# Which engine makes four 128x512 sums of the hidden blocks in 13 of 48 units of a two-layer network on one core

## Chip, cores and metric

The kernel runs on one core of one Trainium2 chip. The metric is the device time of one execution in microseconds, lower is better. Three runs of the kernel before took 1935.4, 1935.69 and 1937.14 us (median 1935.69).

## Reference, cut to what matters

```python
x = x + L0(x, itok_B_0_2, wi, wo, swi, swo, g1, g2)    # x: (2, 2048, 512) float32
x = x + (einsum('bsd,bdh->bsh', x, W[cat]) + b[cat])   # one 512x512 matrix for each batch entry

def L0(x, label, wi, wo, swi, swo, g1, g2):            # D = 512, F = 2048
    s0 = relu(x @ swi[0]) @ swo[0]                     # shared network 0
    s1 = relu(x @ swi[1]) @ swo[1]                     # shared network 1
    eo = relu(x @ wi[label]) @ wo[label]               # chosen by a label for each batch entry
    w = softmax(relu(concat(eo[:, 0], s0[:, 0], s1[:, 0]) @ g1) @ g2)
    return eo * w[0] + s0 * w[1] + s1 * w[2]
```

## The kernel before

**Work.** The 4096 tokens are cut into four blocks ("supers") of 1024, the hidden width of each of the three networks into four slices of 512. One super, network and slice make a unit N; there are 4 x 12 = 48. The two products of a unit (up into the hidden layer, down out of it) are done by a seven-product scheme for 2x2 blocks: instead of eight block products, seven products of sums of blocks. The up product is done in two halves, n = 2N and 2N+1, of seven products each; the down product has seven for both halves together. Each operand is split into a high part (rounded, made by ScalarE, "ACT") and a low part (the remainder, made by VectorE, "DVE"), and TensorE ("PE") runs three matmuls for each tile pair: high by high, high by low, low by high.

**Hidden blocks.** Of each half, ACT and DVE bring four hidden blocks out of PSUM: `relu_11`, `relu_12`, `block_22` with `relu_22`, `block_21` with `relu_21`. DVE's `block_22` adds a copy `w` to a bank and writes `hid` (line 1332); `block_21` adds a copy `u` and writes `HT` (line 1341). The down products need four sums of these blocks, made by `hidden_sum` (line 772, its instruction in line 790): sum 0 = h22 - h12, sum 1 = sum 0 + h11, sum 2 = h12 - h11, sum 3 = h21 - sum 1. Each is 128x512 for one half. In every unit but unit 0, GpSimd ("POOL") makes the four sums of half 0 and DVE those of half 1. `sums_made` (line 766) names the semaphore and the count that tell of a sum; ACT's `hidden_high` and DVE's `hidden_low` (HH and HL, both halves in one 128x1024 instruction) wait for both halves.

**Weight blocks.** The first time a weight set is used, the kernel makes its sums and its high and low parts on the chip and stores them; later units load them. These are the prepared units: 0 to 11 and 32 to 35. There DVE also makes the sums of the up blocks (`up_sums`, 128x256) and all low parts (`up_low` into WU, `down_low` into WD), ACT all high parts, and GpSimd the four sums of the down blocks (`down_sums`, lines 792 to 807, 128x512, into PDS).

**Order.** There is no planner: each engine has its order written out. A pass m of the loops runs the up products of unit m+1 and the down products of unit m. The prediction calls it step m. In it a = 2(m+1) and b = a + 1 are the two up halves. PE's order is two up products, one down product, and so on seven times. On DVE a step begins with an addition of a down product into ACC (line 1310), then sums 0, 1 and 3 of unit m's half 1, `up_low` of a (late part), `up_sums`, low parts, an addition, sum 2, low parts, `up_low` of b (early part), `block_22(a)`, low parts, an addition, `block_21(a)`. The second half of the step has the same two blocks of b. ACT goes on from `block_21` with `relu_21` (line 952), `relu_12` (line 959) and `first_product` (line 924, a copy of one bank over another, for which a product of PE waits). `up` makes product 1 of a half wait for `block_21` of the half before, product 2 for `first_product`, product 6 for `block_22`.

GpSimd's loop (line 848) in pass m: sum 3 of unit m's half 0; sums 0 and 1 of unit m+1's half 0; two sums of down blocks if unit m+1 is prepared; sum 2; the other two sums of down blocks. So its first sums run in the second half of the step before. A sum may only be written when the down product of the unit before that used its place has been made.

Of the kernel before, what the change touches and what calls it, by code (L numbers as in the profile page):

```python
# [23 lines left out]
STEPS = SUPERS * STEPS_SUPER  # L24
# [37 lines left out]
LO_ORDER_END = [0, 1, 6, 2, 3, 4, 5]  # L62


T_COUNT = [(1, 2, 3, 4), (1, 2, 4, 3)]


def super_of(N):
    return N // STEPS_SUPER


def net_of(N):
    return N % STEPS_SUPER // STEPS_NET
# [6 lines left out]
def prepared(N):  # L80

    return 0 <= N < STEPS and (super_of(N) == 0 or (super_of(N) == 2 and net_of(N) == 2))
# [30 lines left out]
def ends_super(N):  # L113

    return N == 0 or N < STEPS - 1 and N % STEPS_SUPER == STEPS_SUPER - 1


def high_index(N, i):
# [28 lines left out]
def begins(N):  # L147

    return slice_of(N) == 0 and (super_of(N) % 2 == 0 or net_of(N) == 0)
# [11 lines left out]
def add_count(N, i):  # L161

    before = ADDS * (N - BEGUN[N]) + 2 * BEGUN[N]
    return before + ({4: 1, 5: 2}[i] if begins(N) else i)


def begin_count(N, i):
    return SUMS * BEGUN[N] + BEGINS[i]
# [44 lines left out]
def build(nc, xT, expert_id, category_id, wi, wo, swi, swo, g1, g2, W, bias, out):  # L213
# [13 lines left out]
    with ctx:  # L227
        def sem(name):
            return ctx.enter_context(nc.semaphore(name))
# [124 lines left out]
        s_T = [sem("hidden_sums_0"), sem("hidden_sums_1")]  # L354
# [393 lines left out]
        def ahead_sum(eng, s, q):  # L748

            done = 4 * (s - 1)  # L750
            if q == 0:
                eng.wait_ge(s_al, 48 * s)
                dst, x, y, op = XS[:, 2, :], XS[:, 2, :], XS[:, 1, :], ALU.subtract
            elif q == 1:
                eng.wait_ge(s_aT, done + 1)
                dst, x, y, op = XS[:, 1, :], XS[:, 1, :], XS[:, 0, :], ALU.subtract
            elif q == 2:
                eng.wait_ge(s_aT, done + 2)
                dst, x, y, op = XS[:, 0, :], XS[:, 2, :], XS[:, 0, :], ALU.add
            else:  # L760
                eng.wait_ge(s_al21, 16 * s)
                eng.wait_ge(s_aT, done + 3)
                dst, x, y, op = XS[:, 1, :], XS[:, 1, :], XS[:, 0, :], ALU.subtract
            eng.tensor_tensor(dst, x, y, op).then_inc(s_aT, 1)

        def sums_made(N, half, which):

            if half == 0 and N > 0:
                return s_T[0], 4 * (N - 1) + T_COUNT[0][which]
            return s_T[1], 4 * N + T_COUNT[1][which]  # L770

        def hidden_sum(eng, N, half, which):

            before = PRODUCTS * (N - 1)
            part = half if N > 0 else slice(0, 2)
            h11, h12, h22 = (hid[:, q, part, :] for q in range(3))
            if N > 0:
                eng.wait_ge(s_dn, before + (3, 2, 4, 5)[which] + 1)
            if which == 0:
                eng.wait_ge(s_relu, 4 * (2 * N + half) + 4)  # L780
                dst, p, q, op = HT[:, 3, part, :], h22, h12, ALU.subtract
            elif which == 1:
                eng.wait_ge(*sums_made(N, half, 0))
                dst, p, q, op = HT[:, 2, part, :], HT[:, 3, part, :], h11, ALU.add
            elif which == 2:
                dst, p, q, op = HT[:, 4, part, :], h12, h11, ALU.subtract
            else:
                eng.wait_ge(*sums_made(N, half, 1))
                dst, p, q, op = HT[:, 5, part, :], HT[:, 1, part, :], HT[:, 2, part, :], ALU.subtract
            eng.tensor_tensor(dst, p, q, op).then_inc(s_T[half], 1)  # L790
# [43 lines left out]
        @block.gpsimd  # L834
        def _(pool):
            def category_identity(b):
                pool.wait_ge(s_wc, 16 * (b + 1))
                for k in range(KD):
                    diag = Wc[:, k, k * P:(k + 1) * P]
                    pool.tensor_tensor(diag, diag, ident[:, :], ALU.add).then_inc(s_wci, 1)  # L840

            pool.memset(ones[:, :], 1.0).then_inc(s_ones, 1)
            pool.memset(ident[:, :], 0.0).then_inc(s_idz, 1)
            pool.wait_ge(s_idz, 1)
            pool.affine_select(out=ident[:, :], in_=ident[:, :], compare_op=ALU.not_equal, fill=1.0,
                               base=0, pattern=[[-1, P]], channel_multiplier=1).then_inc(s_ident, 1)
            pool.wait_ge(s_ident, 1)
            for m in range(STEPS):
                N, d = m + 1, m
                if m > 0:  # L850
                    hidden_sum(pool, d, 0, 3)
                if m in (19, 20):
                    for q in range(3):
                        ahead_sum(pool, m - 17, q)
                if N < STEPS:
                    hidden_sum(pool, N, 0, 0)
                    hidden_sum(pool, N, 0, 1)
                if prepared(N):
                    down_sums(pool, N, False)
                if N < STEPS:  # L860
                    hidden_sum(pool, N, 0, 2)
                if m in (19, 20):
                    ahead_sum(pool, m - 17, 3)
                if prepared(N):
                    down_sums(pool, N, True)
                if m in (STEPS_SUPER, 3 * STEPS_SUPER):
                    category_identity(m // (2 * STEPS_SUPER))

        @block.scalar
        def _(act):  # L870
# [55 lines left out]
            def seventh_product(n):  # L926
                act.wait_ge(s_up, PRODUCTS * n + 2)
                if n > 2:
                    act.wait_ge(s_ev, 2 * (n - 3) + 1)
                act.activation(w[:, :], ups[2][:, :], ACT.Copy).then_inc(s_w, 1)  # L930
# [30 lines left out]
            def hidden_high(N, i):  # L961

                relus = 4 * (2 * N + 1)
                if i in (0, 6):
                    act.wait_ge(s_relu, relus + (2 if i == 6 else 1 if N > 0 else 3))
                    if N > 0:
                        act.wait_ge(s_dn, PRODUCTS * (N - 1) + i + 1)
                    src = hid[:, 0 if i == 0 else 2, :, :]
                else:
                    if i == 1:  # L970
                        act.wait_ge(s_relu, relus + (3 if N > 0 else 4))
                    else:
                        for half in range(2):
                            act.wait_ge(*sums_made(N, half, {3: 0, 2: 1, 4: 2, 5: 3}[i]))
                    src = HT[:, i, :, :]
                act.activation(HH[:, i, :, :], src, ACT.Copy).then_inc(s_hhi, 1)  # L976

            def first_down_product(N):

                for j in range(2):  # L980
                    if j == 1:
                        act.wait_ge(s_dn, PRODUCTS * N + 1)
                    else:
                        act.wait_ge(s_d0, N + 1)
                        act.wait_ge(s_warm, 1)
                        if N > 0:
                            if begins(N - 1):
                                act.wait_ge(s_acp, begin_count(N - 1, 6))
                            else:
                                act.wait_ge(s_acc, add_count(N - 1, 6))  # L990
                    act.activation(rps[1][:, j, :], rps[0][:, j, :], ACT.Copy).then_inc(s_pc, 1)
# [91 lines left out]
            for m in range(STEPS):  # L1083
                N, d = m + 1, m
# [63 lines left out]
                if start:  # L1148
                    token_high(s + 1, 4)
                    token_high(s + 1, 5)  # L1150
                    seventh_product(a)
                    token_high(s + 1, 6)
                    hidden_high(d, 3)
                    chain(a)
                    hidden_high(d, 6)
                    first_down_product(d)
                    hidden_high(d, 2)
                    made(m - 1, PRODUCTS - 1)
                    second(0)
                    relu_11(a)  # L1160
                else:
                    hidden_high(d, 3)
                    if more:
                        seventh_product(a)
                    made(m - 1, PRODUCTS - 1)
                    hidden_high(d, 2)
                    second(0)
                    if more:
                        chain(a)
                    hidden_high(d, 6)  # L1170
                    if more:
                        relu_11(a)
                    first_down_product(d)
                if d > 0 and super_of(d) % 2 == 1 and rel == 1:
                    scale_sums(d)
                if prepared_half(b):
# [760 lines left out]
```

## Time and profile before

| | |
|---|---|
| median of three runs | 1935.69 us |
| the profiled execution | 1937.22 us |
| its span, first to last instruction | 1935.3 us |
| TensorE busy | 1928.5 us (100%), 8494 matmuls |
| VectorE busy | 1354.5 us (70%), 1522 instructions |
| ScalarE busy | 979.7 us (51%) |
| GpSimd busy | 384.9 us (20%), 271 instructions |
| granted TensorE clock | 1.00 |

The busy shares are averages over the whole. The prepared units lie in the first 480 us and between about 1240 and 1440 us; there VectorE's share is far above its mean. A PE pause is too short to show in the shares. It shows in the length of a step, in the list of waits, and in the timeline as idle time before a matmul.

### The profile page before, as it was taken

Reading aid. Unit: us, or ns where it says so; the run is one execution under the profiler, and the core shown is the slowest. Engines: PE = TensorE matmul, PEld = TensorE weight load, DVE = VectorE, ACT = ScalarE, POOL = GpSimd, SP = SyncE. Lnnn points to the kernel's source line nnn. Section 1 sums busy time; section 2 is a strip of 40 time slices with the busy share of each in tenths; the row PEclk is TensorE's granted clock in tenths of the full one; section 3 lists DMA queues with packets and bytes.
Section 4 is the critical chain, followed back from the end, with each engine's and each line's share of the span. In section 5 each row is a group of like instructions: output and inputs, shape, how many; then the busy total and the mean of one; then the engine's idle time right before and its main releaser. Section 6 shows DMA issues by size and latency. Waiting matters only on the chain. (4 is left out here: it accounts for less than half of the span.)

```text
span 1935.3 us, 25260 instructions
## 1 busy us (share of the span) xinstructions
PE 1928.5 (100%) x8494; PEld 1592.9 (82%) x8494; DVE 1354.5 (70%) x1522; ACT 979.7 (51%) x1440; POOL 384.9 (20%) x271
## 2 busy tenths in 40 slices
PE   9999999999999999999999999999999999999999
PEld 8877888888888888888888888888888888888887
DVE  8999988898566556565655545588986656555566
ACT  7666766766554333444554344456566434344342
POOL 0342234223111111331111111122321112111120
PEclk9999999999999999999999999999999999999999
DMA  6868787867877666786776676578778676656642
GB/s 234 318 244 308 303 297 280 294 237 306 305 248 227 204 216 194 275 292 221 255 251 216 194 223 204 193 277 298 268 291 290 222 236 222 214 184 211 224 157 98
DMA packets 193170, 470.91 MB, mean 243 GB/s; under 512 B 17044, under 2 KB 58004, under 8 KB 186900
## 3 DMA queue, kind: packets, MB, share of 16 engines
q1 hardware_dynamic: 193044, 469.31, 70.5%
q8 instruction: 70, 1.15, 0.2%
q14 instruction: 56, 0.46, 0.1%
HBM read 322.44 MB, written 146.80 MB: 242 GB/s over the span
## 5 line engine op out<-in xcount | busy, mean ns | idle before, releaser
L1735 PE MATMUL rps<-HH,WD 128*128 128x512 f32 x2672 | 876.5, 389 | 0.0
L1735 PE MATMUL ups<-XH,WU 128*128 128x512 f32 x2632 | 865.7, 389 | 1.8 <-DVE hid L1332 1.0
L1735 PEld LDWEIGHTS rps<-HH,WD 128*128 128x128 f32 x2672 | 501.4, 188 | 105.0 <-issue 0.5
L1735 PEld LDWEIGHTS ups<-XH,WU 128*128 128x128 f32 x2632 | 494.1, 188 | 108.4 <-DVE hid L1332 3.1
L1735 PE MATMUL rps<-HL,WD 128*128 128x512 f32 x1336 | 519.7, 389 | 0.0
L1735 PE MATMUL ups<-XL,WU 128*128 128x512 f32 x1316 | 512.0, 389 | 0.0
L790 POOL TENSOR_TENSOR HT<-hid 128x512 f32<-128x512 f32 x94 | 128.0, 1362 | 1313.0 <-PE rps L1735 1313.0
L1291 DVE TENSOR_TENSOR HL<-HT,HH 128x1024 fp32r<-128x1024 f32 x240 | 290.2, 1218 | 10.5 <-ACT HH L976 5.3
L1313 DVE SCALAR_TENSOR_TENSOR ACC<-rps,gw,ACC 128x1024 f32<-128x1024 f32 x126 | 161.5, 1282 | 191.1 <-PE rps L1735 190.9
L1735 PEld LDWEIGHTS rps<-HL,WD 128*128 128x128 f32 x1336 | 250.8, 188 | 51.9
L1735 PEld LDWEIGHTS ups<-XL,WU 128*128 128x128 f32 x1316 | 246.9, 188 | 50.8
L976 ACT ACTIVATE HH<-HT 128x1024 fp32r<-128x1024 f32 x240 | 252.3, 1053 | 35.4 <-DVE HT L790 34.0
L1310 DVE TENSOR_TENSOR ACC<-rps,ACC 128x1024 f32<-128x1024 f32 x124 | 151.3, 1220 | 92.5 <-PE rps L1735 92.1
L952 ACT ACTIVATE HT<-HT 128x512 f32<-128x512 f32 x94 | 59.4, 632 | 267.6 <-DVE HT L1341 267.6
L1291 DVE TENSOR_TENSOR HL<-hid,HH 128x1024 fp32r<-128x1024 f32 x96 | 130.9, 1363 | 20.7 <-ACT HH L976 20.7
L1332 DVE TENSOR_TENSOR hid<-ups,w 128x512 f32<-128x512 f32 x94 | 64.7, 688 | 112.0 <-PE ups L1735 111.9
L944 ACT ACTIVATE hid<-ups 128x512 f32<-128x512 f32 x94 | 55.9, 595 | 111.3 <-PE ups L1735 111.3
L936 ACT ACTIVATE u<-ups 128x512 f32<-128x512 f32 x94 | 56.2, 598 | 100.7 <-PE ups L1735 100.7
L930 ACT ACTIVATE w<-ups 128x512 f32<-128x512 f32 x94 | 55.3, 588 | 97.6 <-PE ups L1735 97.6
L976 ACT ACTIVATE HH<-hid 128x1024 fp32r<-128x1024 f32 x96 | 101.6, 1059 | 3.5 <-PE rps L1735 2.0
L924 ACT ACTIVATE ups<-ups 128x512 f32<-128x512 f32 x94 | 54.8, 583 | 80.7 <-PE ups L1735 77.6
L948 ACT ACTIVATE hid<-hid 128x512 f32<-128x512 f32 x94 | 59.4, 632 | 69.9 <-DVE hid L1332 69.9
(153 smaller groups left out, 1549.1 us busy)
## 6 DMA issues: line engine op xcount, KB each, us to landing
WU<-wu_kept SPq DMA_DIRECT2D x448, 256.0 KB, 3.4
WD<-wd_kept SPq DMA_DIRECT2D x224, 512.0 KB, 3.4
wd_kept<-WD SPq DMA_DIRECT2D x112, 512.0 KB, 4.2
wu_kept<-WU SPq DMA_DIRECT2D x30, 1024.0 KB, 4.9
wu_kept<-WU SPq DMA_DIRECT2D x30, 768.0 KB, 4.5
sums_kept<-ACC SPq DMA_DIRECT2D x28, 512.0 KB, 5.7
MB<-sums_kept SPq DMA_DIRECT2D x28, 512.0 KB, 5.7
XS<-in_x_dram SPq DMA_DIRECT2D x21, 512.0 KB, 6.1
```

Of the source, the lines that this page charges most:

```text
L790: eng.tensor_tensor(dst, p, q, op).then_inc(s_T[half], 1)
L930: act.activation(w[:, :], ups[2][:, :], ACT.Copy).then_inc(s_w, 1)
L936: act.activation(u[:, :], ups[1][:, :], ACT.Copy).then_inc(s_u, 1)
L944: act.activation(hid[:, 0, half, :], ups[0][:, :], ACT.Relu).then_inc(s_relu, 1)
L948: act.activation(hid[:, 2, n % 2, :], hid[:, 2, n % 2, :], ACT.Relu).then_inc(s_relu, 1)
L952: act.activation(HT[:, 1, n % 2, :], HT[:, 1, n % 2, :], ACT.Relu).then_inc(s_relu, 1)
L976: act.activation(HH[:, i, :, :], src, ACT.Copy).then_inc(s_hhi, 1)
L1291: dve.tensor_tensor(HL[:, i, :, :], src, HH[:, i, :, :].bitcast(F32), ALU.subtract).then_inc(s_hlo, 1)
L1310: dve.tensor_tensor(ACC[:, j, :, :], src[:, :, :], ACC[:, j, :, :], ALU.add).then_inc(s_acc, 1)
L1313: dve.scalar_tensor_tensor(out=ACC[:, j, :, :], in0=src[:, :, :], scalar=gw[:, g:g + 1], in1=ACC[:, j, :, :], op0=ALU.mult, op1=ALU.add).t ...
L1332: dve.tensor_tensor(hid[:, 2, half, :], ups[1][:, :], w[:, :], ALU.add).then_inc(s_ev, 1)
L1735: ins = pe.matmul(dst, stationary[a], moving[c], start=start and j == 0, stop=stop and j == 2, skip_group_check=True)
```

## The change

`in_one(N, which)` is true for unit 0 and for prepared units that don't end a super: units 1 to 10 and 32 to 34. For these, `hidden_sum` on DVE takes both halves in one 128x1024 instruction, and GpSimd's calls are left out. Unit 11 and unit 35 (they end a super) and all loaded units keep the split. `BY_HALVES` counts the sums that GpSimd still makes. On ACT, `relu_11(a)`, which waits for sum 2 of the unit before, is put behind `first_down_product(d)`, where d = m, in all steps but those that start a super.

```diff
-T_COUNT = [(1, 2, 3, 4), (1, 2, 4, 3)]
+T_COUNT = (1, 2, 4, 3)
...
+def in_one(N, which):
+
+    return N == 0 or prepared(N) and not ends_super(N)
+
+
+BY_HALVES = [sum(not in_one(n, which) for n in range(1, N) for which in range(4)) for N in range(STEPS + 1)]
...
         def sums_made(N, half, which):
 
-            if half == 0 and N > 0:
-                return s_T[0], 4 * (N - 1) + T_COUNT[0][which]
-            return s_T[1], 4 * N + T_COUNT[1][which]
+            if half == 0 and not in_one(N, which):
+                return s_T[0], BY_HALVES[N] + which + 1
+            return s_T[1], 4 * N + T_COUNT[which]
 
         def hidden_sum(eng, N, half, which):
 
             before = PRODUCTS * (N - 1)
-            part = half if N > 0 else slice(0, 2)
+            part = slice(0, 2) if in_one(N, which) else half
...
             for m in range(STEPS):
                 N, d = m + 1, m
-                if m > 0:
+                if not in_one(d, 3):
                     hidden_sum(pool, d, 0, 3)
...
-                if N < STEPS:
+                if N < STEPS and not in_one(N, 0):
                     hidden_sum(pool, N, 0, 0)
                     hidden_sum(pool, N, 0, 1)
                 if prepared(N):
                     down_sums(pool, N, False)
-                if N < STEPS:
+                if N < STEPS and not in_one(N, 2):
                     hidden_sum(pool, N, 0, 2)
...
                     hidden_high(d, 6)
+                    first_down_product(d)
                     if more:
                         relu_11(a)
-                    first_down_product(d)
```

## Rows read from the trace of the kernel before

**Rows 1.** Busy time by step; per engine busy us (count), then clock, DMA share, GB/s

```profile
104.60:144.60 40.00, 39.19 (x169) 31.21 (x169) 39.27 (x50) 23.50 (x39) 13.13 (x9) 1.00 0.68 257
144.60:184.40 39.80, 39.19 (x170) 31.25 (x169) 38.06 (x46) 22.92 (x39) 12.49 (x9) 1.00 0.88 325
184.40:222.70 38.30, 38.30 (x169) 31.47 (x169) 36.37 (x47) 26.90 (x44) 12.08 (x9) 1.00 0.80 302
...
298.80:336.90 38.10, 38.10 (x169) 31.55 (x169) 33.69 (x45) 23.92 (x38) 12.01 (x9) 1.00 0.82 304
```

**Rows 2.** Waits of PE's weight loads, 100 to 205 us: total, times, longest

```profile
PEld ups L1735 <- DVE hid L1332: 3.1, 5, 0.8
PEld ups L1735 <- DVE WU L1271: 1.2, 2, 0.7
PEld ups L1735 <- ACT ups L924: 0.7, 2, 0.3
```

**Rows 3.** Timeline of step 2, DVE and POOL: start, us, engine, line, operation

```profile
131.77 1.29 POOL L790 TENSOR_TENSOR HT<-hid 128x512 f32<-128x512 f32 x1 [26.16 <-PE rps L1735]
131.83 1.78 DVE L1278 TENSOR_TENSOR WD<-PDS,WD 128x512 fp32r<-128x512 f32 x1
...
134.97 1.77 DVE L1271 TENSOR_TENSOR WU<-PUS,WU 128x512 fp32r<-128x512 f32 x1
...
136.66 1.21 DVE L1310 TENSOR_TENSOR ACC<-rps,ACC 128x1024 f32<-128x1024 f32 x1
```

**Rows 4.** Operations on tile HT, whole span: ns min/median/max

```profile
L1291 DVE TENSOR_TENSOR HL<-HT,HH x240: 1210/1218/1227, 37.1 to 1902.9; 128x1024 fp32r<-128x1024 f32 x120
L790 DVE TENSOR_TENSOR HT<-hid x96: 674/684/1702, 31.3 to 1893.4; 128x512 f32<-128x512 f32 x94, 128x1024 f32<-128x1024 f32 x2
```

**Rows 5.** Timeline of step 7, first half: DVE, ACT and PE

```profile
297.48 1.23 DVE L1310 TENSOR_TENSOR ACC<-rps,ACC 128x1024 f32<-128x1024 f32 x1 [1.04 <-PE rps L1735]
298.62 0.79 DVE L790 TENSOR_TENSOR HT<-hid 128x512 f32<-128x512 f32 x1
...
300.91 0.69 DVE L1271 TENSOR_TENSOR WU<-PUR,WU 128x512 fp32r<-128x512 f32 x1
...
303.85 0.61 PE L1735 MATMUL ups<-XH,WU 128*128 128x512 f32 x2
...
311.06 0.68 DVE L1332 TENSOR_TENSOR hid<-ups,w 128x512 f32<-128x512 f32 x1
...
313.60 0.39 PE L1735 MATMUL ups<-XH,WU 128*128 128x512 f32 x1
...
316.26 0.68 DVE L1341 TENSOR_TENSOR HT<-ups,u 128x512 f32<-128x512 f32 x1
...
318.18 0.58 ACT L924 ACTIVATE ups<-ups 128x512 f32<-128x512 f32 x1
...
320.17 0.62 PE L1735 MATMUL ups<-XH,WU 128*128 128x512 f32 x2
```

**Rows 6.** Timeline of step 3: a pause of PE that `block_22` ends

```profile
159.69 0.68 DVE L1332 TENSOR_TENSOR hid<-ups,w 128x512 f32<-128x512 f32 x1
...
160.43 0.50 PE L1735 MATMUL ups<-XH,WU 128*128 128x512 f32 x1 [0.33 <-DVE hid L1332]
```

**Rows 7.** Timeline of step 34: first sum on DVE, copy on ACT, product on PE

```profile
1370.95 1.70 DVE L790 TENSOR_TENSOR HT<-hid 128x512 f32<-128x512 f32 x1
...
1391.42 0.58 ACT L924 ACTIVATE ups<-ups 128x512 f32<-128x512 f32 x1
...
1392.50 0.62 PE L1735 MATMUL ups<-XH,WU 128*128 128x512 f32 x2
```

**Rows 8.** Timeline of DVE at the start of steps 1 and 5

```profile
66.34 1.63 DVE L790 TENSOR_TENSOR HT<-hid 128x512 f32<-128x512 f32 x1
...
68.08 1.60 DVE L790 TENSOR_TENSOR HT<-HT,hid 128x512 f32<-128x512 f32 x1
...
222.46 1.23 DVE L790 TENSOR_TENSOR HT<-hid 128x512 f32<-128x512 f32 x1
```

## The prediction

> **What bounds the kernel now.** I read the table by stretches first, cut where the up products of consecutive steps begin. TensorE (PE) is busy all of step 7, 38.10 of 38.10 us, at full clock [rows 1]. A change on VectorE (DVE) and GpSimd (POOL) can therefore move the time only by adding or removing PE pauses, and I look for those. Step 2 takes 40.00, step 3 takes 39.80, step 4 takes 38.30 against the 38.10 [rows 1]: 1.9 + 1.7 + 0.2 = 3.8 us of pauses. The weight load's waits of those steps name `hid` of line 1332 (`block_22`), WU of line 1271 (`up_low`), both DVE, and the ACT copy of line 924 (`first_product`), which comes behind DVE's `block_21` [rows 2]. DVE is busy 39.27 of 40.00 us in step 2 [rows 1]: there it is the bound. In step 7 it has 4.4 us of idle and PE loses nothing. So 3.8 us is about all that this change can win.
>
> **Why DVE is full.** In step 2, GpSimd's sum starts at 131.77 and runs 1.29 us; DVE's `WD<-PDS,WD` starts at 131.83 and takes 1.78 us, ending 0.5 after GpSimd ends. `WU<-PUS,WU` at 134.97 takes 1.77 [rows 3]. The same form alone takes 0.68 to 0.69, as at 300.91 [rows 5], so each meeting costs DVE 1.1 us. The addition from PSUM at 136.66 takes its plain 1.21 beside a busy GpSimd [rows 3]: only operations with both inputs in SBUF are held up. The page "SBUF — State Buffer" of the Trainium skill, section "Who interferes with whom", says that a VectorE instruction with two SBUF inputs contends with a GpSimd instruction that reads SBUF, and that whoever is first holds the port pair for the whole instruction. The trace agrees: 1.1 us is a whole remainder of a 1.3 us GpSimd instruction, not a shared rate.
>
> **What changes.** Units 1 to 10 and 32 to 34, 13 of 48. Call step m the pass in which unit m's sums are finished by DVE.
>
> (a) *Removed from GpSimd:* four 128x512 sums per unit, 1.29 us and more each [rows 3]. Three come in the second half of the step before; the fourth at the step's start. In steps 1 to 3 DVE's stretched instructions of the second half add about 5.5 us; in step 2 six, the largest 1.1 each, two of which are shown [rows 3]. The four weight-block sums stay. They no longer queue behind two hidden sums, so they start about 3 us earlier, when the last low part of the unit before is there. I walk them by alternation: the first blocks WU for 1.1, the second falls beside an ACC addition from PSUM, the third blocks HL for 0.8, the fourth is beside ACC and `block_21`. Kept: about 2.0. Saved: 3.5 per step where DVE is late. Bounds: 0 (the same number of meetings) and 5.5 (none). I take 3.5, since the PSUM operations there, about 1.2 us long, are nearest to the length of a GpSimd sum.
>
> (b) *Added to DVE:* four sums become 128x1024. A 128x1024 subtraction from SBUF takes 1.218 against 0.684 for 128x512 [rows 4]: +0.53 each, 2.15 for the four. The fixed part is paid once, as before. The 104 ns between dependent sums stay. All four stand before `block_22(a)` and `block_21(a)` in DVE's order, three of them also before `up_low(a, late)`.
>
> (c) *What that delays.* In step 7 the chain starts at 297.48, where ACC had waited 1.04 us for PE; from there to `block_21` (316.26 to 316.94) DVE has no idle but the fixed 0.1s [rows 5]. Being early before is worth nothing, since PE releases the chain; the 2.15 go through whole, less what GpSimd's fourth sum stretches now. `HT<-hid` took 0.79 for 0.68 in step 7, and 1.70 in step 34 [rows 5, 7]: 0.1 and 1.0 come back. `block_22` ends at 311.74 and PE begins the product that waits for it at 313.60, 1.9 later [rows 5]. `block_21` ends at 316.94, ACT's copy at 318.76, and PE's product (second matmul of the pair at 320.17) begins at 320.40: 1.6 [rows 5]. When PE does stall, its start follows the supplier by 0.06 (160.37 to 160.43) and its first matmul takes 0.50 for 0.39 [rows 6], so 0.2 of any margin is not usable. In step 34 the copy ends at 1392.00 and the product begins at 1392.73: 0.5 usable [rows 7].
>
> Steps 6 to 10 read like this have usable margins of 1.5, 1.5, 1.1, 0.8, 0.5; steps 32 to 34 have 0.7, 0.8, 0.5 (eight steps; the second and the last shown). The delays are 2.07, 2.04, 1.75, 1.83, 1.13 and 1.32, 1.70, 1.13: 2.15 less the stretch saved, and less about 0.25 in steps 8 and 9 and 0.1 in 33, where DVE waits for ACT today. Differences: 0.57 + 0.54 + 0.65 + 1.03 + 0.63 + 0.62 + 0.90 + 0.63 = 5.6 us of new pauses. Steps 1, 4 and 5 have margin left: in 1 and 5 the sums at the start are stretched today (1.63, then 1.23 for 0.68 [rows 8]; in step 1 a second one as much), in 4 today's delay at its start goes. `up_low(a, late)`'s first part ends at 301.60 and its product begins at 304.07 [rows 5]: 2.5 us against 1.6.
>
> (d) *Steps 2 to 4.* Per step DVE gains 3.5 and pays 2.15, so the lateness does not build up; but the start chain of (c) applies with a usable 1.6 against 2.15, and step 2 has three more additions of first blocks. I take 0.55 in step 2, 0.7 in step 3, 0 in step 4: 1.25 for 3.8, a gain of 2.5.
>
> (e) *The swap on ACT:* `relu_11(a)` now waits for DVE's sum 2 (its end moves from 307.3 to about 309.4). Behind it stand `up_high(b, early)`, a weight high part and HH; `up_high` moves by 1.2 us while DVE, which uses it, moves by 2.1. Cost 0. The copies of rps stand before it and move by 0.5, less than `block_22` does. Without the swap they would wait with it. Bounds 0 and 1.2 per step.
>
> (f) *SyncE:* stores of WU and WD wait for DVE's low parts, so they and the block loads behind them issue up to 2 us later, in the first half of a step; the loads are used a half step later. Cost 0; bounds 0 and 1 us in all. Semaphore counts change nothing in time.
>
> **Sum.** +5.6 − 2.5 = +3.1 us. Against the profiled execution, 1937.2 us with 1935.3 of span and 1.9 around it, that is 1940.3. That execution lay 1.5 above the median of the three runs, 1935.69; on the median the forecast is **1938.7 us**.
>
> **Rivals.**
> 1. *The port decides.* VectorE's total falls wherever GpSimd was in its way, the pauses of steps 2 to 4 end, and the start chain's margins turn out to be enough because DVE reaches the start earlier. Price −3.8 + 1.5 = −2.3, at best −3.8: 1931.9 to 1934.5. For it: 5.5 us of stretch per step, more than the 2.15 added. Against it: ACC's wait of 1.04 for PE just before the chain. It decides if the chain of step 7 shows idle time after its start. Chance 0.17.
> 2. *The weight sums take over the blocking (slower).* Started 3 us earlier, they meet WU, WU, HL and WD in place of the hidden sums, nothing is saved in steps 2 to 4, and 2.15 is added in each of them: 3 x 2.15 + 5.6 = 12, 1947.7; with half the saving about 1943. It decides once the saving per step is below 2.15. For it: every meeting costs 1.1 whatever GpSimd computes. Against: half as many GpSimd instructions, and three PSUM operations between. Chance 0.13.
> 3. *It cancels.* The sums are dearer by 2.15 and the late steps gain as much as the others lose; the pauses only move: 1935.7, no change. Chance 0.12.
> The forecast's case has 0.58, and its own range, from ±0.25 us in each of eight margins and 2 us in (a), is 1936.5 to 1941.
>
> About 0.2%, 3.9 us, is what a measurement of this kernel can tell from no change. The forecast is just inside. Slower by more: a third of its own case (0.19), the second rival, and a little of the SyncE and ACT bounds (0.03): 0.35. Faster by more needs nearly all of the 3.8 us: 0.05. Within: 0.60. The range takes in most of the first rival and the half of the second: 1934.0 to 1943.0.
>
> **What would show it.** GpSimd has 52 fewer instructions; DVE's `HT` sums of 13 units are 128x1024 at 1.22. The stretches of steps 2 and 3 fall by 3.0 to 3.5 us each. The windows of steps 2 and 3 shorten to about 38.7, and those of steps 6 to 10 lengthen from 38.1 to between 38.6 and 39.1, with PE waits named for `hid` (1332) and ACT's copy (924), at the middle of the step. Wrong would be: steps 6 to 10 still at 38.1 (then margins or chain were misread), or steps 2 to 4 still at 40 (then (a) was).

## The result, and the profile after

The changed kernel takes 1939.76 us in the median of 20 runs, the kernel before 1936.80 in 20: a ratio of 1.0016, 95% interval 1.0010 to 1.0022, so +3.0 us (1.9 to 4.3). The prediction said +3.1 us, written as 1938.7 on the median of three runs shown then; 1935.69 + 3.1 is 1938.8. Over 20 runs the kernel before is at 1936.8, and the same sum then gives 1939.9. All executions of the variants below ran at a granted TensorE clock of 1.00, except one of `order_alone` (3265 us at 0.56), which is left out of its median.

The page's busy line of the changed kernel:

```profile
PE 1931.8 (100%) x8494; PEld 1592.4 (82%) x8494; DVE 1354.2 (70%) x1522; ACT 979.8 (51%) x1440; POOL 310.8 (16%) x219
```

GpSimd has 52 instructions fewer. VectorE does 52 halves of sums more and is busy for the same 1354 us: the longer sums add 52 x 0.53 = 28 us, and it loses about as much less to GpSimd. The shares say nothing more; the steps do. Busy time by step of the changed kernel (columns as in [rows 1]): steps 2, 3, 4, 7, 9 and 34.

```profile
104.70:143.40 38.70, 38.63 (x169) 31.39 (x169) 37.74 (x51) 24.52 (x41) 6.68 (x4) 1.00 0.78 290
143.40:182.00 38.60, 38.54 (x169) 31.34 (x168) 35.22 (x45) 23.42 (x38) 6.47 (x4) 1.00 0.83 313
182.00:220.50 38.50, 38.37 (x170) 31.46 (x169) 34.95 (x45) 26.43 (x41) 6.46 (x4) 1.00 0.80 301
...
297.30:335.90 38.60, 38.53 (x169) 31.34 (x168) 35.61 (x45) 23.67 (x38) 6.65 (x4) 1.00 0.79 291
...
374.60:413.40 38.80, 38.62 (x169) 31.34 (x168) 36.63 (x48) 24.25 (x39) 6.99 (x4) 1.00 0.71 265
...
1373.50:1412.10 38.60, 38.54 (x169) 31.35 (x168) 33.66 (x39) 23.99 (x37) 11.93 (x8) 1.00 0.75 286
```

Steps 2 and 3, 40.0 and 39.8 us before [rows 1], are down to 38.7 and 38.6. Step 7, free of pauses before, is up to 38.6, and all of steps 6 to 10 and 32 to 34 are like it. GpSimd is busy 6.7 us in step 2 instead of 13.1.

The waits of PE's weight loads in the changed kernel from 60 to 460 us (answering [rows 2]) name the two deadlines of the prediction, `block_22` (`hid`) and the copy behind `block_21` (ACT `ups`), now in nearly every step. `block_21` itself (`HT`) is waited for once, in step 9, and `up_low` (WU) is gone from the list:

```profile
PEld ups L1743 <- DVE hid L1340: 3.5, 7, 0.6
PEld ups L1743 <- ACT ups L932: 2.5, 7, 0.6
PEld ups L1743 <- DVE HT L1349: 0.4, 1, 0.4
```

Step 7 of the changed kernel in the timeline (answering [rows 5]; line numbers have shifted: `block_22` is now 1340, `block_21` 1349, the copy 932):

```profile
295.94 1.23 DVE L1318 TENSOR_TENSOR ACC<-rps,ACC 128x1024 f32<-128x1024 f32 x1 [1.63 <-PE rps L1743]
297.08 1.22 DVE L798 TENSOR_TENSOR HT<-hid 128x1024 f32<-128x1024 f32 x1
...
311.55 0.68 DVE L1340 TENSOR_TENSOR hid<-ups,w 128x512 f32<-128x512 f32 x1
...
312.28 0.19 PEld L1743 LDWEIGHTS ups<-XH,WU 128*128 128x128 f32 x1 [0.49 <-DVE hid L1340]
...
312.28 0.50 PE L1743 MATMUL ups<-XH,WU 128*128 128x512 f32 x1
312.62 0.40 PE L1743 MATMUL ups<-XL,WU 128*128 128x512 f32 x1
...
316.75 0.68 DVE L1349 TENSOR_TENSOR HT<-ups,u 128x512 f32<-128x512 f32 x1
...
318.66 0.58 ACT L932 ACTIVATE ups<-ups 128x512 f32<-128x512 f32 x1
...
319.30 0.19 PEld L1743 LDWEIGHTS ups<-XH,WU 128*128 128x128 f32 x1 [0.34 <-ACT ups L932]
```

From the start of ACC to the end of `block_22` it was 311.74 - 297.48 = 14.26 us [rows 5]; now it is 312.23 - 295.94 = 16.29: 2.03 later, where 2.04 was forecast. `block_21` likewise (19.46 and 21.49). Ahead of the chain DVE waits for PE longer than before, 1.63 instead of 1.04 us. Its last two low parts before that wait took 1.28 us instead of 2.44, so the freed port did make it early, and PE's release takes that away. Then PE waits twice in the step, for `block_22` and for the copy behind `block_21`.

Step 2 of the kernel before, three lines more beside [rows 3]:

```profile
133.53 1.52 DVE L1271 TENSOR_TENSOR WU<-PUR,WU 128x256 fp32r<-128x256 f32 x1
134.72 1.47 POOL L805 TENSOR_TENSOR PDS<-PDR 128x512 f32<-128x512 f32 x1
136.27 1.63 POOL L807 TENSOR_TENSOR PDS<-PDS,PDR 128x512 f32<-128x512 f32 x1
```

Step 2 of the changed kernel (answering [rows 3]):

```profile
131.24 0.68 DVE L1286 TENSOR_TENSOR WD<-PDS,WD 128x512 fp32r<-128x512 f32 x1
131.84 0.42 DVE L1279 TENSOR_TENSOR WU<-PUR,WU 128x256 fp32r<-128x256 f32 x1
132.06 1.34 POOL L813 TENSOR_TENSOR PDS<-PDR 128x512 f32<-128x512 f32 x1 [31.93 <-DVE WD L1286]
132.17 1.78 DVE L1279 TENSOR_TENSOR WU<-PUS,WU 128x512 fp32r<-128x512 f32 x1
133.48 1.63 POOL L815 TENSOR_TENSOR PDS<-PDS,PDR 128x512 f32<-128x512 f32 x1
133.88 1.21 DVE L1318 TENSOR_TENSOR ACC<-rps,ACC 128x1024 f32<-128x1024 f32 x1
...
135.08 1.50 POOL L806 TENSOR_TENSOR PDS<-PDR 128x512 f32<-128x512 f32 x1
...
135.94 1.71 DVE L1299 TENSOR_TENSOR HL<-hid,HH 128x1024 fp32r<-128x1024 f32 x1
136.53 2.28 POOL L808 TENSOR_TENSOR PDS<-PDR,PDS 128x512 f32<-128x512 f32 x1
```

The four weight-block sums meet DVE nearly as walked: WU pays 1.1, the second falls beside the PSUM addition, HL pays 0.5 (0.8 was forecast), the fourth costs DVE nothing and is itself held up by HL. WD and the small WU, stretched to 1.78 and 1.52 before, take their plain 0.68 and 0.42. I call stretch what a VectorE instruction takes beyond the undisturbed time of its form (0.42, 0.68 or 1.22 us). Over all VectorE instructions that start between 40 and 240 us it adds up to 27.1 us before and 9.3 after. In steps 2 and 3 it falls from 5.5 and 5.6 to 1.6 and 1.7. In steps 6 to 8 together it does not fall: 5.7 us before, 6.3 after.

### The profile page after: what moved, and what is told of

The parts are those of the page before. It is cut to its first block and busy times, and to the rows that moved or that the text cites. A ratio compares the mean times of both kernels' runs of the same rounds, so it can differ in the third digit from the quotient of the medians.

```text
span 1938.0 us, 25169 instructions
## 1 busy us (share of the span) xinstructions
PE 1931.8 (100%) x8494; PEld 1592.4 (82%) x8494; DVE 1354.2 (70%) x1522; ACT 979.8 (51%) x1440; POOL 310.8 (16%) x219
## 5 line engine op out<-in xcount | busy, mean ns | idle before, releaser
L798 POOL TENSOR_TENSOR HT<-hid 128x512 f32<-128x512 f32 x68 | 93.3, 1372 | 964.6 <-PE rps L1743 964.6
L999 ACT ACTIVATE rps<-rps 128x512 f32<-128x512 f32 x96 | 54.8, 581 | 88.1 <-PE rps L1743 64.8
```

## Experiments

All differences are of medians, against the kernel before on the same chip (1936.25 to 1936.48). Step lengths are those between the first up products of two steps in the trace. The sum of all step lengths agrees with the medians within 1 us. Steps 12 and 36 take 38.7 and 38.6 in the kernel before and are within 0.1 of that in every variant; of the other steps named here, one that is free of pauses takes 38.1.

**1 and 2. Each half of the units alone.**

```diff
 def in_one(N, which):
-    return N == 0 or prepared(N) and not ends_super(N)
+    return N == 0 or N > 5 and prepared(N) and not ends_super(N)     # late_units
+    return N == 0 or N <= 5 and prepared(N) and not ends_super(N)    # early_units
```

> Only units 6 to 10 and 32 to 34 have their sums on VectorE; units 1 to 5 are split as before. Theory (the longer chain at the start of a step, which TensorE releases, costs where VectorE is not late): the pauses of steps 2 to 4 stay at 3.8 us, and steps 6 to 10 and 32 to 34 lengthen from 38.1 to 38.6 to 38.9 us, together +5.0; step 35 gives back 0.2. So +4.8 us against the kernel before, ratio 1.0025. Rival (the freed port decides in every step): no more than before, ratio 1.000 or below.

1941.51 us, +5.0; ratio 1.0028 (1.0017 to 1.0038), as expected.

> The other part alone: units 1 to 5 on VectorE, units 6 to 10 and 32 to 34 split as before. Theory: steps 2 and 3 shorten from 40.0 and 39.8 to about 38.7, step 4 lengthens by 0.2, later steps stay at 38.1: -2.2 us against the kernel before, ratio 0.9989. Rival (the weight sums of GpSimd block in place of the hidden sums): nothing is saved, +2 to +6 us.

1934.24 us, −2.2; ratio 0.9988 (0.9979 to 0.9997), as expected. Steps 2, 3, 7 and 9 of the kernel with units 6 to 10 and 32 to 34 only:

```profile
104.10:144.00 39.90, 39.19 (x169) 31.21 (x168) 39.17 (x50) 23.48 (x39) 13.03 (x9) 1.00 0.69 257
144.00:183.80 39.80, 39.23 (x169) 31.23 (x169) 38.06 (x46) 22.93 (x39) 12.48 (x9) 1.00 0.87 328
298.80:337.50 38.70, 38.63 (x169) 31.39 (x169) 35.68 (x45) 23.68 (x39) 6.62 (x4) 1.00 0.79 293
376.10:415.00 38.90, 38.71 (x170) 31.42 (x169) 36.74 (x48) 24.24 (x39) 7.00 (x4) 1.00 0.72 265
```

and with units 1 to 5 only:

```profile
104.80:143.40 38.60, 38.54 (x169) 31.32 (x168) 37.66 (x51) 24.50 (x40) 6.68 (x4) 1.00 0.76 286
143.40:182.10 38.70, 38.63 (x170) 31.42 (x169) 35.33 (x45) 23.45 (x38) 6.47 (x4) 1.00 0.84 315
296.80:334.80 38.00, 38.00 (x169) 31.47 (x168) 34.38 (x45) 23.89 (x38) 12.19 (x9) 1.00 0.82 304
372.90:411.00 38.10, 38.10 (x170) 31.55 (x169) 36.20 (x46) 24.02 (x39) 11.99 (x9) 1.00 0.72 257
```

The change is two changes. Each part does in its steps what the whole does there, and nothing in the other's; +5.0 and −2.2 add to 2.8, the whole's 3.0 within noise. The exception is step 35, which belongs to neither: it takes 38.8 before, 38.6 in the whole and with the late units, and 38.2 with the early units only. No run tells why.

**3. Without the swap on ScalarE.** `relu_11(a)` back ahead of `first_down_product(d)`.

> The changed kernel with ScalarE's relu_11(a) put back ahead of the copies of rps. Theory: the copies then end about 1.7 us later, with 0.3 us left before TensorE needs the first, so nothing is lost: +3.0 us against the kernel before, ratio 1.0015, as with the swap. Rival (the swap hides a wait that the moved sum 2 brings): up to 1.2 us more in each of 10 steps, +4 to +15 us.

1939.56 us, +3.1; ratio 1.0017 (1.0008 to 1.0026). No step differs by over 0.05 us from the change's. The swap is worth nothing.

**4. Port freed, chain not longer.** GpSimd's sums of half 0 in the 13 units are left out and made nowhere, so the result is not the reference's.

```diff
-            part = slice(0, 2) if in_one(N, which) else half
+            part = slice(0, 2) if N == 0 else half
...                                             # high and low parts of sums, in the 13 units:
+                    src = HT[:, i, 1:2, :].to_broadcast([P, 2, TB])
```

> Leaves work out: in the 13 units GpSimd makes no hidden sums and VectorE makes half 1 only (128x512, as before); the high and low parts of the four sums read half 1 twice. So the port is freed and the start chain is not lengthened. Theory: all pauses of steps 2 to 4 go and none come elsewhere, -3.8 us against the kernel before, ratio 0.998; steps 2, 3 and 6 to 10 all at 38.1. Rival (the pauses come from VectorE's own load, not from the port): steps 2 and 3 stay above 39, -1 us or less.

1932.28 us, −4.2; ratio 0.9979 (0.9970 to 0.9988). Steps 2, 3 and 7:

```profile
103.80:141.90 38.10, 38.10 (x170) 31.55 (x169) 35.77 (x51) 24.77 (x40) 6.67 (x4) 1.00 0.77 290
141.90:180.00 38.10, 38.10 (x170) 31.55 (x169) 33.03 (x45) 23.83 (x38) 6.46 (x4) 1.00 0.89 334
294.20:332.30 38.10, 38.10 (x170) 31.55 (x169) 32.38 (x45) 23.84 (x38) 6.04 (x4) 1.00 0.83 304
```

Steps 1 to 11 and 32 to 35 have no pause. To free the port is enough to end those of steps 2 to 4, since VectorE's own work is here what it was before. A rival would be that GpSimd's sums came late for others; but in the kernel before, neither VectorE nor ScalarE waits for GpSimd between 60 and 460 us. About 4 us is then also the most that this choice of engine can win.

**5. Long chain, port kept busy.**

```diff
+        def as_before(eng, N, which):       # in GpSimd's loop where hidden_sum was left out
+            eng.wait_ge(s_dn, PRODUCTS * (N - 1) + (3, 2, 4, 5)[which] + 1)
+            if which == 0:
+                eng.wait_ge(s_relu, 4 * (2 * N) + 4)
...
+            eng.tensor_tensor(scratch, same, same, ALU.subtract).then_inc(s_scr, 1)
```

> The changed kernel, but GpSimd still runs a 128x512 subtraction with both inputs in SBUF at each place where its sum was left out (it reads a constant tile and writes a scratch tile that nobody reads: added work). The chain is long and the port stays busy. Theory (two separate effects): VectorE's stretches of steps 1 to 4 are back at 23 us; steps 2 to 4, full already, lengthen by up to 2.15 each, and steps 6 to 10 and 32 to 34 reach 38.7 to 39.7: +15 us against the kernel before (+10 to +19), ratio 1.008. Rival (the port does not matter, only the chain): +3 us, as the change.

1949.16 us, +12.9; ratio 1.0066 (1.0052 to 1.0080). Steps 2, 3 and 7:

```profile
105.50:146.80 41.30, 39.12 (x169) 31.25 (x169) 40.57 (x51) 24.21 (x41) 11.48 (x9) 1.00 0.72 268
146.80:187.90 41.10, 38.88 (x169) 31.30 (x168) 39.36 (x47) 23.18 (x39) 11.23 (x9) 1.00 0.84 310
303.50:342.50 39.00, 38.59 (x169) 31.38 (x169) 37.26 (x45) 23.67 (x39) 11.37 (x8) 1.00 0.81 303
```

VectorE's stretch from 40 to 240 us is back at 21.4 of the 27.1 us, and the same VectorE program takes 10 us more. Here too VectorE never waits for GpSimd between 60 and 460 us, so it is not the weight-block sums, now later, that hold it up. The two effects are separate: instructions on GpSimd whose data nobody reads cost TensorE 2.6 us in step 2 alone (41.3 against 38.7). Against the kernel before, step 2 is 1.3 us longer, not the 2.15 that I took at most. The whole, +12.9, lies in the expected range, and the rival's +3 does not fit.

**6 and 7. The same work at another place.** All sums on VectorE, those of half 0 as 128x512 in the second half of the step before, only sum 3 in one at the start:

```diff
-    return N == 0 or prepared(N) and not ends_super(N)
+    return N == 0 or prepared(N) and not ends_super(N) and (which == 3 or N == 1)
...
                 second(4)
+                if by_vector(N):                    # split_in_time; in split_late these
+                    hidden_sum(dve, N, 0, 0)        # two stand behind block_21(b)
+                    hidden_sum(dve, N, 0, 1)
...
                 block_21(b)
+                if by_vector(N):
+                    hidden_sum(dve, N, 0, 2)
```

> VectorE makes all sums of the 13 units, but those of half 0 where GpSimd made them: sums 0, 1 and 2 as 128x512 instructions in the second half of the step before, where VectorE waits for TensorE from step 5 on; only sum 3 is 128x1024 at the start of the step (unit 1 keeps all four in one). VectorE's own work per step is 0.2 us more than in the changed kernel; the chain at the start grows by 0.54 instead of 2.15. Theory (the place of the added work decides): steps 6 to 10 and 32 to 34 back at 38.1, steps 2 and 3 at 38.1 to 38.5: -3 us against the kernel before (-2 to -4), ratio 0.9984. Rival (the amount of added work decides): no better than the change, +3 us or more.

1940.36 us, +4.1; ratio 1.0021 (1.0012 to 1.0030): a miss. Steps 4 to 8, 10 and 34 are free of pauses (38.1), as the place of the work predicts, but step 1 takes 39.4, step 2 40.3, step 3 38.8, step 32 38.3 and steps 9 and 33 40.0. Step 9 of this kernel shows why:

```profile
405.27 1.82 POOL L811 TENSOR_TENSOR PDS<-PDR 128x512 f32<-128x512 f32 x1
405.87 1.77 DVE L803 TENSOR_TENSOR HT<-hid 128x512 f32<-128x512 f32 x1
407.05 1.72 POOL L813 TENSOR_TENSOR PDS<-PDR,PDS 128x512 f32<-128x512 f32 x1
407.74 1.58 DVE L803 TENSOR_TENSOR HT<-HT,hid 128x512 f32<-128x512 f32 x1
409.25 0.68 DVE L1345 TENSOR_TENSOR hid<-ups,w 128x512 f32<-128x512 f32 x1
...
409.98 0.19 PEld L1753 LDWEIGHTS ups<-XH,WU 128*128 128x128 f32 x1 [2.05 <-DVE hid L1345]
```

I had put two sums right where GpSimd's weight sums run, and right ahead of `block_22(b)`, for which TensorE waits. They took 3.4 us instead of 1.4.

> As split_in_time, but sums 0 and 1 of half 0 stand behind block_21(b) instead of ahead of block_22(b). In split_in_time TensorE waited up to 2.0 us for block_22(b), behind two sums that GpSimd's weight sums stretched to 1.77 and 1.58 us; the starts of the steps were free of pauses. Theory (the place decides, and block_22(b) was the one in the way): steps 6 to 10 and 32 to 34 at 38.1 to 38.2, steps 2 and 3 at 38.1 to 38.6, -3 us against the kernel before (-2 to -4.3). Rival (VectorE's total, 0.2 us a step above the changed kernel's, is what costs): +3 to +4 us.

1934.15 us, −2.3; ratio 0.9989 (0.9980 to 0.9998), inside the expected range. Behind `block_21(b)` the same sums take 0.68 and 0.69. Steps 4 to 10, 33 and 34 are at 38.1, steps 2 and 3 at 38.7 and 38.8. Between these two kernels nothing differs but the place of two instructions in VectorE's order: 6.2 us, by the step lengths as well.

**8 and 9. Only the order.**

```diff
                     hidden_low(d, 2)
-                    made(m, 0)
                     ...
                     block_22(a)
+                    made(m, 0)              # where half b is prepared
...
+                if early:                   # prepared unit that ends no super
+                    block_21(a)
                 if d >= 0:
                     hidden_low(d, 4)
                 second(2)
```

> The changed kernel with two moves in VectorE's order: the weight low part behind sum 2 goes behind block_22(a), and block_21(a) goes ahead of the low part of sum 2 and an addition. Same instructions, same total. Theory (block_22 and block_21 are late by 0.4 and 0.6 us in each step): both pauses go, -3.5 us against the kernel before (-2.5 to -4.2), ratio 0.998. Rival (VectorE's total bounds the step): +3 us as with the change.

1934.99 us, −1.3; ratio 0.9994 (0.9985 to 1.0003), not told apart from the kernel before and a miss: −3.5 was expected. It is 4.3 us below the change, though.

> The kernel before with the same two moves and its sums still split between the engines. Theory: in steps 2 to 4 VectorE has 0.7 us of idle in 40, its total bounds them, so the order helps little: -1 us (0 to -2), ratio 0.9995; steps 6 to 10 stay at 38.1. Rival (the order alone is what is worth having): -3.5 us, as much as together with the moved sums.

1935.46 us, −0.8; ratio 0.9996 (0.9986 to 1.0005), the same. Its step 2 is still 39.4 and step 3 38.7: where VectorE is full, the order helps in part. It wins 1.9 us in steps 2 to 4 and loses 0.7 in steps 10 and 11. Steps 2, 3, 7, 11 and 35 of blocks_first:

```profile
104.20:142.20 38.00, 38.00 (x169) 31.48 (x168) 37.52 (x51) 24.80 (x40) 6.63 (x4) 1.00 0.77 287
142.20:180.30 38.10, 38.10 (x170) 31.55 (x169) 35.36 (x45) 24.01 (x38) 6.09 (x4) 1.00 0.82 308
294.60:332.60 38.00, 38.00 (x169) 31.48 (x168) 35.22 (x45) 23.77 (x38) 5.43 (x4) 1.00 0.75 274
447.20:486.10 38.90, 38.46 (x169) 31.72 (x170) 32.16 (x36) 24.29 (x35) 6.10 (x5) 1.00 0.77 292
1406.10:1446.30 40.20, 38.78 (x170) 31.67 (x170) 32.75 (x37) 24.73 (x37) 6.67 (x5) 1.00 0.75 279
```

Moving two instructions takes both pauses out of the steps where the change had put them, with VectorE's work unchanged; only step 8 keeps 0.3 us, for `block_22`. But 2.2 us of the gain come back as pauses in steps 11 and 35, at the start of a token block, where `block_21(b)` stands behind the low part of a token operand. ScalarE waits there for the operand's load, and the load is behind a store in SyncE's order.

**10 to 12. Where the rest went.** `blocks_first_tokens` puts `block_21(b)` ahead of that low part, `tokens_alone` does the same to the kernel before, `blocks_first_but_last` leaves `made(m, 0)` in place in the last step before a token block.

> As blocks_first, and in the last step before a new token block VectorE makes block_21(b) ahead of the low part of a token operand, which waits for a load. In blocks_first steps 1 to 10 and 32 to 34 were at 38.1 but step 11 took 38.9 and step 35 took 40.1, with TensorE waiting for block_21(b), which stood behind that low part. Theory (that place is where the rest of the gain went): steps 11 and 35 back to 38.1, -4.0 us against the kernel before (-3.3 to -4.5), ratio 0.998. Rival (the token load's delay comes back at another wait): -1.3 us, as blocks_first.

1935.62 us, −0.9; ratio 0.9996 (0.9987 to 1.0005). The rival held: steps 11 and 35 are at 39.3 and 39.8, and TensorE now waits for the low part XL and for a copy by ScalarE. In this kernel ScalarE's waits from 430 to 460 us, and SyncE's below:

```profile
ACT XH L891 <- DMA XT<-xT_kept: 5.5, 2, 5.1
```

```profile
SPq L481 <- DMA wu_kept<-WU: 6.9, 1, 6.9
```

SyncE waits for the landing of a store of WU before it issues the load of that set, and the token loads stand behind it in its queue. In the kernel before the same wait was 4.7 us. The store is not issued later than there: 22.7 us after the start of step 10 in `blocks_first` and 22.9 in the kernel before. It lands later, 10.2 us after its issue instead of 7.5.

> The kernel before with that one move of block_21(b) ahead of the token low part. Theory: step 35 from 38.8 to 38.1, step 11 unchanged at 38.1: -0.6 us (0 to -1), ratio 0.9997. Rival (the token load itself is late for TensorE): no change of any step.

1936.14 us, −0.3; ratio 0.9999 (0.9990 to 1.0008). Step 35 goes from 38.8 to 38.1 and step 11 stays, as said; so small a gain is not told apart in the medians.

> As blocks_first (VectorE's low part of the token operand ahead of block_21(b), as in the kernel before), but in the last step before a new token block (10 and 34) the weight low part stays where it was. In blocks_first that move put SyncE's stores and the loads behind them later in these steps, and step 11 took 38.9 and step 35 took 40.1. Theory (the moved low part delays the store, and the store the token load): steps 11 and 35 at 38.1 to 38.8, a pause of up to 0.4 at block_22 in steps 10 and 34, -3.2 us against the kernel before (-2.4 to -4), ratio 0.9983. Rival (the token load runs at the DMA queues' own time, so whatever TensorE gains in the steps before it is lost there): steps 11 and 35 together still 2 us over, -1.3 us.

1934.70 us, −1.8; ratio 0.9988 (0.9979 to 0.9997), less than the −2.4 to −4 expected. Steps 1 to 9, 32 and 33 are at 38.1, steps 10 and 34 at 38.5 and 38.4, step 11 at 38.2 and step 35 at 39.0. By its steps it is 2.7 us shorter; step 35 alone has 0.9 of pauses left. So both theories hold in part: with the low part back in its place the store lands 9.0 us after its issue, and steps 11 and 35 are within 0.2 of the kernel before (38.1 and 38.8), but 35 gains nothing either. Why the store takes longer to land, and whether a busier DMA queue is behind it, no run here tells.

Three kernels beat both the kernel before and the change: split_late, units 1 to 5 only, and this one. Their intervals overlap; none is shown best. Against the version that left work out, about 2 us at most are still to be had.

## Why the prediction was right, step by step

- **What bounds (right).** Pauses of PE were all that moved. left_out is 4.2 us faster by the medians and 4.5 by the steps: the 3.8 that were read from steps 2 to 4, and 0.7 in step 35, which the prediction leaves out (38.8 before, 38.1 in left_out, 38.6 in the change). It gives 0.2 of the change's time back.
- **(a) Port relief (right in place, a little small).** Forecast: 3.5 us saved per step where DVE is late, 2.0 kept. In steps 2 and 3, 3.9 were saved in each and 1.6 and 1.7 kept, mostly since HL paid 0.5 and not 0.8. Over 40 to 240 us, five steps, it is (27.1 − 9.3) / 5 = 3.6 saved, 1.9 kept. Experiments 4 and 5 show it from both sides.
- **(b), (c) The longer chain (right).** 2.15 less 0.11 forecast for step 7, 2.03 measured. The new pauses by step, forecast and measured: step 6 0.57, 0.58; step 7 0.54, 0.58; step 8 0.65, 0.57; step 9 1.03, 0.77; step 10 0.63, 0.58; step 32 0.62, 0.59; step 33 0.90, 0.77; step 34 0.63, 0.58. Sum 5.6 and 5.0. The terms too large are those of steps 9 and 33: there ACC to the end of `block_21` grew by 1.53, not by 1.83 and 1.70, as waits for ACT took up more than the 0.25 and 0.1 allowed.
- **(d) Steps 2 to 4 (right in sum, one step missed).** Forecast gain 2.5: 38.65 and 38.8 in steps 2 and 3, nothing in step 4. Measured 38.66, 38.67 and 38.51: gains 1.35 and 1.11, and step 4 loses 0.26. The prediction counted on the late start of step 4 going away. It went, but only by 1.88 us (ACC began 0.72 after the step's start before and begins 1.16 ahead of it now), while the chain grew by 2.14. The one wait of PE there is for `hid`, 0.6 us. So 2.2 instead of 2.5.
- **Sum.** +5.0 − 2.2 − 0.2 (step 35) = +2.6 by steps, +3.0 by the medians, +3.1 forecast. The new pauses came out 0.6 lower than forecast, the gain 0.3 lower, and the 0.2 of step 35 was not forecast: by the steps the sum is 0.5 too high. That the medians say +3.0 and so meet the forecast within 0.1 is in part luck; their interval is 1.9 to 4.3.
- **(e) The swap (right):** nothing, by experiment 3. **(f) SyncE (right here, wrong as a rule):** it cost nothing in the change, but once the other pauses were gone, the load behind a store took 2 us back in experiment 8. The prediction gave it a bound of 1.
- **Rivals.** The first (port decides everywhere) fell with the pauses of steps 6 to 10 and 32 to 34: DVE's earlier start was lost in the 1.63 us that it waits ahead of its chain. Its price of −2.3 us comes to 1933.4, though its range is written up to 1934.5. The second fell where it mattered, with 3.9 us saved in each of steps 2 and 3 against 2.15 added. In steps 6 to 8 its picture did come true, and nothing was saved; but there DVE has time to spare ahead of the chain, which PE releases. The third had the right kind of picture, gains and losses in different steps, but not their sizes.

## What to carry to other kernels

A move of work between engines has a price at each place, not one price: read which instruction releases the chain that the new work stands in, and how far each consumer behind it is from its deadline. Time won ahead of a releasing wait is worth nothing; of time added behind it, all that exceeds the smallest margin is lost. With a move of work, look also at the order on the engine that gets it: alone the order brought nothing that could be told apart, but two instructions moved in the changed kernel brought 4.3 us, more than the move itself had cost. And look at the next wait that a faster step will meet; here it was a load behind a store.

## What the runs showed of the hardware

- A GpSimd subtraction of 128x512 from SBUF, about 1.3 us long, costs VectorE up to 1.1 us (0.68 became 1.78) in instructions with two SBUF operands, and nothing (1.21) in those that read PSUM. That it does so for data that have nothing to do with VectorE's is shown by experiment 5. It works the other way round too: the GpSimd sum at 136.53 in step 2 of the changed kernel, which began while HL ran, took 2.28 us.
- The stretch depends on which instructions meet, not only on how many run. With half of GpSimd's instructions gone, two thirds of it went between 40 and 240 us (27.1 to 9.3), but none in steps 6 to 8 (5.7 to 6.3). And the same two sums of VectorE took 3.4 us at one place and 1.4 at another, with the same work on GpSimd (experiments 6 and 7).
- TensorE's restart after a pause costs about 0.1 us beyond the wait: the first matmul is recorded as 0.50 instead of 0.39, and the second starts 0.34 us behind it (312.28 to 312.62 in step 7 of the changed kernel) instead of 0.23. All pauses of step 3 before and of step 7 after show it.
